# First attention of a fused block: the first score fill set between the halves of the projection, the second and third moved up

## What is computed

```
x = x + tanh(g_xattn[0]) * attention(layernorm(x), ctx, ...)

q = concat(ctx, xn) @ Wq          # 32 heads of 8
k, v = xn @ Wk, xn @ Wv           # 8 key heads of 8
sk, sv = ctx @ Wsk, ctx @ Wsv
kcat, vcat = concat(sk, k), concat(sv, v)      # 256 keys
scores = q kcat^T / sqrt(8) + alibi, masked to a window of 64 (ctx) or 32 (x) keys
out = softmax(scores) @ vcat @ Wo
x = x + tanh(g_ffn[0]) * top2_of_8_experts(layernorm(x))
...  (three more pairs of layers)
```

## Time and profile before

| | |
|---|---|
| median of 3 runs | 1187.99 us (1187.56 to 1189.01) |
| the profiled execution, its own time | 1181.77 us |
| its span, first to last instruction | 1180.0 us |
| busy in the span: PE / DVE / ACT / POOL | 1029.3 / 807.8 / 588.3 / 600.4 us |
| mean granted TensorE clock | 0.954 of 2.4 GHz |
| first attention with its scores, L888 | first at 29.1 us, last at 285.6 us |

### The profile page before, as it was taken

The page is one execution under the profiler, slowest core; times in us unless marked ns, Lnnn a source line. Parts: engine busy times, 40 slices in busy tenths (PEclk is TensorE's granted clock), DMA queues, the critical chain, the costliest instruction groups (busy, mean ns, idle before and its releaser), DMA issues.

```text
span 1180.0 us, 30765 instructions
## 1 busy us (share of the span) xinstructions
PE 1029.3 (87%) x11053; PEld 808.9 (69%) x11053; DVE 807.8 (68%) x2187; ACT 588.3 (50%) x1354; POOL 600.4 (51%) x1158
## 2 busy tenths in 40 slices
PE   4798998998889668888899979999978789979898
PEld 2576766766689624444577756777756579979898
DVE  2576666666647558888688885888865766756475
ACT  2454645655566347776621105777742544347432
POOL 2453555564588788874221124777733626510461
PEclk8899989999889959999999997999979999989999
DMA  5332323335388755543110010111002701246231
GB/s 177 104 105 87 121 82 123 105 107 162 119 262 256 183 155 146 148 135 113 40 72 0 1 43 24 35 35 35 15 11 84 232 32 46 73 137 196 90 113 59
DMA packets 110189, 119.85 MB, mean 102 GB/s; under 512 B 13372, under 2 KB 94484, under 8 KB 109788
## 3 DMA queue, kind: packets, MB, share of 16 engines
q1 hardware_dynamic: 85660, 79.42, 22.4%
q0 software_dynamic: 8256, 22.08, 6.1%
q10 hardware_dynamic: 16128, 16.43, 4.2%
HBM read 68.85 MB, written 49.03 MB: 100 GB/s over the span
## 4 chain that ended last, share of the span: by engine, by line
PE 46%; DVE 24%; POOL 11%; issue 11%; ACT 4%; DMA 2%; ACTq 1%; POOLq 0%; SPq 0%; DVEq 0%
PE psum L1125 4%; DVE mx L2460 3%; DVE mx L888 3%; DVE x L2254 3%; PE psum L2564 2%; DVE mx L2761 2%; PE psum L1057 2%; PE psum L1108 2%; PE psum L1758 2%; PE psum L1059 2%; PE psum L1088 2%; PE psum L1760 2%; PE psum L1759 2%; PE psum L1180 2%; POOL rstd L790 1%
## 5 line engine op out<-in xcount | busy, mean ns | idle before, releaser
L888 DVE TENSOR_REDUCE mx<-psum 128x6 f32<-128x960 f32 (+3 forms) x80 | 80.7, 1008 | 64.8 <-PE psum L1093 63.6
L788 POOL TENSOR_SCALAR veps<-mv 128x1 f32<-128x1 f32 x112 | 28.8, 257 | 187.2 <-DVE mv L775 136.0
L766 POOL DMA_INDIRECT got<-ys,rows_y x64 | 64.2, 1002 | 89.4 <-DMA ys<-yt 66.6
L975 ACT ACTIVATE PT<-psum 128x1024 f32<-128x1024 f32 x64 | 65.5, 1024 | 64.8 <-PE psum L1113 64.8
L2460 DVE TENSOR_REDUCE mx<-psum 128x4 f32<-128x1024 f32 x64 | 77.0, 1205 | 22.3 <-PE psum L2537 22.3
L2501 ACT ACTIVATE PT<-psum 128x512 f32<-128x512 f32 x128 | 69.5, 595 | 19.6 <-PE psum L2548 18.1
L1758 PE MATMUL psum<-xnTh,w7h 128*128 128x256 f32 x256 | 74.4, 291 | 1.3 <-issue 0.7
L1760 PE MATMUL psum<-xnTh,w7l 128*128 128x256 f32 x256 | 72.4, 283 | 0.0
L2858 ACT ACTIVATE PT<-psum,mx 128x128 f32<-128x128 f32 x256 | 69.8, 396 | 5.1 <-DVE mx L2761 5.1
L790 POOL TENSOR_TENSOR rstd<-veps,minus_half 128x1 f32<-128x1 f32 x112 | 67.6, 604 | 9.3
L1759 PE MATMUL psum<-xnTl,w7h 128*128 128x256 f32 x256 | 72.3, 283 | 0.0
(11 more groups left out here) (445 smaller groups left out, 3412.6 us busy)
## 6 DMA issues: line engine op xcount, KB each, us to landing
xs<-qpad SPq DMA_DIRECT2D x34, 512.0 KB, 3.4
PT<-xs SPq DMA_DIRECT2D x78, 128.0 KB, 2.9
ys<-yt ACTq DMA_DIRECT2D x78, 128.0 KB, 2.5
ext<-qscr SPq DMA_DIRECT2D x96, 64.0 KB
arena<-in_w SPq DMA_DIRECT2D x16, 320.0 KB, 3.0
w_raw<-in_w SPq DMA_DIRECT2D x12, 384.0 KB, 4.4
q_parts<-kscr SPq DMA_DIRECT2D x66, 64.0 KB, 2.4
kvd<-arena ACTq DMA_DIRECT2D x16, 256.0 KB, 3.0
```

The costliest lines, as they stand in the source:

```text
L888: V.tensor_reduce(mx0[:, u0:u0 + m].rearrange("p j e -> p e j"), src, axis=AX.X, op=ALU.max, negate=True).then_inc(F("mx").sem, 1)
L975: A.activation(PT[:, 1024 * r:1024 * (r + 1)], bank(6, 2), ACT.Exp).then_inc(F("p").sem, 1)
```

## The change

On PE, `project` is cut in two, `project_rows` (xn's weights) and `project_context` (the context's), and fill 0 of block n, which was in the next turn between K0 and L1150, is set between them, with its waits for the transposed q and k of that block and, new, for the copy of the maxima of block b (the fill writes the bank in which these stood). Fill 1 takes its old place behind K0. Fill 2 goes ahead of the transposes of o_n (L1161). On DVE, maxima 1 go ahead of `normalise`. No instruction is added or taken away other than waits; all arithmetic stays.

```diff
@@ DVE body @@
                 if even:
                     steps(t // 2 - 1, (7,))
+                if among(b):
+                    maxima(b, 1)
                 if among(pp):
                     normalise(pp)
-                if among(b):
-                    maxima(b, 1)
                 if even:
                     steps(t // 2 - 1, (8,))
@@ PE @@
-            def project(m, s, turn):
-                wait(f"ctx_loaded{s}", turn, 16)
+            def project_rows(m, s):
                 wait("xnT", m, 1)
                 for c in range(NC):
                     MM(bank(0)[:, 128:512], xnT[:, s, c, 0:T], w0x[:, c], start=(c == 0), stop=False, skip_group_check=True)
+
+            def project_context(m, s, turn):
+                wait(f"ctx_loaded{s}", turn, 16)
                 for c in range(NC):
                     t = MM(bank(0)[:, 0:384], ctxT[:, s, c], w0c[:, c], start=False, stop=(c == NC - 1), skip_group_check=True)
                 t.then_inc(F("qkv_psum").sem, 1)
@@ PE body @@
                     key_scores(p, 1 - s, 0)
+                ft = i - 3
                 if among(b):
-                    if isinstance(i, int) and i == 0:
-                        pe.wait_ge(loaded_s0, 32)
-                        pe.wait_ge(loaded_route, LOADS_R)
-                    wait("qkT", b, 3)
-                    scores(b, s, 0)
-                ft = i - 3
+                    scores(b, s, 1)
...
-                if among(b):
-                    scores(b, s, 1)
                 if among(p):
                     key_scores(p, 1 - s, 1)
                 if among(ft):
                     front_transpose(pe, ft)
+                if among(b):
+                    scores(b, s, 2)
                 if among(pp):
                     wait("on", pp, 1)
...
-                if among(b):
-                    scores(b, s, 2)
...
                 if among(m):
-                    project(m, s, half_i + 1)
+                    project_rows(m, s)
+                if among(n):
+                    if n == 0:
+                        pe.wait_ge(loaded_s0, 32)
+                        pe.wait_ge(loaded_route, LOADS_R)
+                    wait("qkT", n, 3)
+                    if among(b):
+                        wait("mxT", b, 1)
+                    scores(n, 1 - s, 0)
+                if among(m):
+                    project_context(m, s, half_i + 1)
```

## The result

| | before | changed |
|---|---|---|
| median of 5 runs | 1187.99 us (1187.56 to 1192.74) | 1178.27 us (1175.59 to 1181.88) |
| ratio | | 0.9925, 95% interval 0.9897 to 0.9953 |
| profiled execution, its own time (span) | 1181.77 (1180.0) us | 1180.07 (1178.3) us |
| mean granted TensorE clock | 0.954 | 0.952 |

Both ratios lie beyond the 0.2% that counts as no change, though the repeat's interval reaches into it.

The account below looks back on a forecast made before the run. PE was taken to bound the stage; 7.1 us paid, less 6.6 in steady turns and 0.7, 0.6, 0.5 at the edges, gave -1.3, taken as -1.1: 1187.99 to 1186.9 us, range 1182.5 to 1190.5.

Parts of the forecast that it names:

- The projection: Fill 0 between the projection's two halves on PE costs 0.51 us a turn, including changes between 128-row and 64-row matmuls.
- The rival of hidden changes: PE loads fill 0's weights during the projection, so fill 0 costs 0.23 us instead of 0.51: 1183.0 us; chance 0.29.
- The window: Between K0 and fill 3, moving fills 1 and 2 early wins 0.51 of PE's 0.86 us wait for DVE each turn.
- the walk: Predicted timeline of one turn from K0: K1 at +1.82, K2 at +3.64, fill 3 at +5.75 us.
- o_n late: Rival: normalise behind maxima 1 makes o_n's transposes late, K2 and all behind slip 0.3 us a turn: 1191; chance 0.17.
- The sum: Over all turns, 7.1 us paid in projections, 6.6 won in steady turns, edge gains besides: -1.3, taken as -1.1 us.
- the edges: Turns 0, 1 and 15, at the stage's ends, win 0.7, 0.6 and 0.5 us.
- The SP weight transfer that follows maxima 1: On SP's queue, it starts up to 1 us earlier in its turn and nobody waits for it; costed at nothing.
- Stalls of PE labelled 'issue': Stalls behind fill 3, as 2.07 us at 148.49, left unchanged; one shifted or lengthened would cost up to 2 us.
- If the stalls move: Last sign that the prediction is wrong: PE's "issue" stalls, taken as unchanged, shift.

Follow-up runs that it names:

- the repeat: The changed kernel, unchanged, timed again with 12 runs against before: 1181.52 us, ratio 0.9963 (0.9938 to 0.9988).
- after_w_on: The changed kernel with the SP weight transfer held until normalise is done, near its old place in the turn: 1189.11 us, ratio 1.0014 to before.
- before_w_late: The kernel before with the SP weight transfer issued after the second clearing transfer, behind maxima 3: 1174.93 us, ratio 0.9900; repeated, 1177.63 us, 0.9915.
- before_again: The kernel before, unchanged, timed and profiled a second time: 1187.33 us, ratio 1.0015 (0.9990 to 1.0041).

## Why the prediction was wrong

**The projection, right.** 0.51 us for fill 0 between the halves: 3.26 measured against 3.25 walked. The rival of hidden changes (0.23) fell; it had 0.29 of the chance, and the changed time came out on its side for a wholly different reason. PE's weight loads in the changed kernel show why nothing was hidden:

```profile
154.39 0.19 PEld L1056 LDWEIGHTS psum<-w_attn,xnT 128*128 128x128 f32 x1
155.12 0.10 PEld L1090 LDWEIGHTS psum<-ext,ohq 64*128 64x128 bf16 x2 [0.55 <-issue]
```

Fill 0's first loads start at 155.12, with its first matmul at 155.13: none ran ahead. The Trainium skill, TensorE: Matmul & The Clock Gate, Step-by-step ①, by which that rival was made, has a weight load pulled ahead of running matmuls under two conditions. The trace doesn't show it at this place, where the height of the tile changes and waits for semaphores stand ahead of the fill; which of the two keeps it back isn't shown.

**The window, right.** K1 waits 0.18 for the exponential (0.28 by the walk, between a shown gap and one by starts), K2 stands at +3.66 for +3.64, fill 3 at +5.77 for +5.75. What held it was the pace of the exponentials. ACT in turn 8 of the changed kernel, the second waiting for K1:

```profile
157.61 1.02 ACT L975 ACTIVATE PT<-psum 128x1024 f32<-128x1024 f32 x1
...
159.44 1.02 ACT L975 ACTIVATE PT<-psum 128x1024 f32<-128x1024 f32 x1 [0.32 <-PE psum L1115]
```

**o_n late, little.** Turns with a place step have K2 at +3.77 to +3.79 (3.65 to 3.7 by the walk) and take 16.00 to 16.02 us: 0.11 to 0.13 over the others, in seven turns, some 0.8 us in all. That is more than the 0.2 taken for it and below the 0.25 a turn from which that rival decides.

**The sum, right for the steady turn and not for the edges.** -1.1 us was forecast for the order of work. Turn 15, with 0.5 to win, is 0.2 longer instead (12.46 to 12.50 us in the changed kernel's profiles, 12.23 and 12.24 in those of before), and turn 14, with the whole gain forecast and only the bare fill to pay, 0.1 longer. With the 0.14 of each turn with a place step, turns without a stall make the stage some 1.3 us longer by the order of work, where the walk has it some 0.8 shorter. Turn 0 can't be read out, as its clock differs between executions. An error of about 2 us, then, less than the intervals resolve and against the gain: it isn't what put the time below the range.

**"The SP weight transfer that follows maxima 1 starts up to 1 us earlier in its turn and nobody in the stage waits for it" was wrong, and is the step that failed.** The shift was read rightly (1.0 to 1.3 us earlier). Somebody waits, though no semaphore ties them: PE, through the fetch of its instructions. It was costed at nothing, and is worth the 4.4 us of the repeat (held back again in after_w_on, the ratio is 1.0014) and more, up to 12 us, when the transfer is moved fully away.

**"Stalls of PE labelled 'issue' ... lie behind fill 3, where the order and the count of instructions before are the same, so I leave them" was wrong as well.** The reason given holds for where in the program the stall stands: behind fill 3 in turn 7 of both kernels. It says nothing of its length, which hangs on when the block arrives. The prediction allowed that a stall could lengthen and cost up to 2 us and the clock; it didn't look for a cause by which it could shorten. "If the stalls move", the last of its signs of being wrong, is the one that came. The two sentences were one: the transfer's move and the stall's length were taken as separate trifles, and one was the cause of the other. The rows for it were in the trace of before: a q8 packet that starts as the weights' packets end, and a stall that ends 2.4 us after it, in several turns.

On fetching, the Trainium skill, Runtime: NRT & Kernel Launch, Instruction fetch mechanics, says that the sequencer fetches blocks of 16 KiB (256 instructions) through a DMA queue of its own, and that the cost of crossing into the next block is mostly hidden. The trace agrees with the first (89 packets for 1.46 MB on the changed kernel's page; stalls whole multiples of 256 PE records apart) and not with the second: PE stood still for 5 to 8 us between 60 and 265 us in before and the changed kernel.

What stays open. No view names the engine for which q8's packets are. That they are PE's rests on two counts: its 76 stalls in the fourteen profiles all end 2.2 to 2.9 us after a packet's start (1.3 to 1.6 after its end), and there is one packet for every 256 PE records. Why the block is asked for at about +4.9 and not earlier isn't shown, nor what the time between the packet's end and PE's next matmul goes into, nor why one stall is followed by 1.2 GHz and another of its length isn't; 2.3 us of stalls were left in before_w_late, and nothing was tried against them. Nor was the split projection combined with another order behind K0.

## What to carry to other kernels

Where PE stands still under "issue", look at the transfer views for the instruction packet that ends it and for the large data transfer right ahead of that packet; moving the one `dma_start` that is in its way (to another point of the turn, at no cost to whoever needs its data) gave 0.8 to 1.0% here (ratios 0.9900 and 0.9915), more than the reordering of PE and DVE, and the same move is worth trying first. When a change moves a step to which a queue is tied (here maxima 1), list the transfers that move with it and what else passes through the DMA engines in that stretch, instructions included. And when a change pays where the walk says it shouldn't, move the suspected transfer alone, both ways (out of the way in the old kernel, back into it in the new one), before crediting the reordering.

## What the runs showed of the hardware

- A fetch of 16 KB of instructions takes its packet 0.9 to 1.8 us. It starts late behind a data transfer: in turns 4 and 7 of before a 320 KB load issued at +3.63 put it at +6.1 to +6.5 instead of +4.9 to +5.0.
- Such stalls of PE, 76 in fourteen profiles, follow each other at 512, 1280 or 1792 PE records, within one, with 2, 5 or 7 instruction packets from one to the next.
- PE's stalls for it end 2.2 to 2.9 us after the packet's start and 1.3 to 1.6 after its end, and were 0.6 to 2.3 us long by starts. After the one of 2.07 us in turn 7 of before the granted clock was 0.50 for the next 4.4 us; after 0.93 us in the changed kernel it stayed at 1.00, and so it did after 1.90 us in turn 4 of before_again. Of the 76, 12 were followed by 1.2 GHz (1.48 to 2.30 us by starts), and eight as long were not. One of 2.3 us cost 5.1 us with the fall (turn 7 at 20.94 against 15.86) and 2.1 without (17.94).
- Setting 64-row matmuls between 128-row ones cost 0.10 us down and 0.12 up again, bfloat16 amid float32. In the new place the change down is 0.10 again (fill 0 stands 1.45 behind L1056's start, where L1059 stood 1.35 behind L1057's), and fill 0 with the change up takes 0.33 for 0.35.
- A wait on a semaphore that holds one transfer back by 0.8 us (+2.66 to +3.43 in turn 7) takes the whole gain of the change away (ratio 1.0014 for 0.9963).
